# The variance of the last layer norm: from VectorE's statistics to a row sum on VectorE and squares on ScalarE

## The reference

```
x = x + layernorm(attn(layernorm(x)))
x = x + layernorm(ffn(layernorm(x)))

layernorm(h) = (h - mean(h)) / sqrt(var(h) + 1e-5)
ffn(x): h   = gelu(x @ ternary(W1).T + b1)      # 512 -> 2048
        out = h @ ternary(W2).T + b2            # 2048 -> 512
```

## Time and profile before

| | |
|---|---|
| median of three runs | 1421.73 us |
| span of the profiled execution, first to last instruction | 1420.3 us |
| TensorE busy | 1400.8 us, 99% |
| VectorE busy | 1116.8 us, 79% |
| ScalarE busy | 878.2 us, 62% |
| GpSimd busy | 422.3 us, 30% |
| granted TensorE clock | 0.999 of full speed |

### The profile page before, as it was taken

One profiled execution on the slowest core, in us unless ns is written; L12 is line 12 of the kernel. 1 busy time (PEld: TensorE's weight loads), 2 busy tenths in 40 slices (PEclk: granted clock), 3 DMA queues, 4 the chain that ended last, 5 costly groups with the idle time before them and its releaser, 6 DMA issues.

```text
span 1420.3 us, 18989 instructions
## 1 busy us (share of the span) xinstructions
PE 1400.8 (99%) x6506; PEld 640.0 (45%) x6506; DVE 1116.8 (79%) x1889; ACT 878.2 (62%) x1264; POOL 422.3 (30%) x522
## 2 busy tenths in 40 slices
PE   7999999999999999999999999999999999999997
PEld 4444444444444444444444444444444444444443
DVE  7999987868779686796867878677796877998744
ACT  7999665656556565675656756565565656753443
POOL 5234241322314232042331413223142321523221
PEclk9999999999999999999999999999999999999999
DMA  8703221211311122121311203113111221001200
GB/s 245 254 36 90 60 83 20 78 30 38 82 30 60 30 61 59 30 66 25 89 30 31 82 16 82 31 38 82 31 60 30 53 67 30 30 1 30 60 31 30
DMA packets 155984, 82.00 MB, mean 58 GB/s; under 512 B 132720, under 2 KB 132720, under 8 KB 155760
## 3 DMA queue, kind: packets, MB, share of 16 engines
q1 hardware_dynamic: 155888, 80.79, 22.0%
HBM read 31.49 MB, written 16.78 MB: 34 GB/s over the span
## 4 chain that ended last, share of the span: by engine, by line
PE 85%; DVE 4%; issue 3%; POOL 1%; ACT 0%; POOLq 0%; DVEq 0%; ACTq 0%
PE f2b L581 14%; PE f2b L582 14%; PE f1b L552 14%; PE f1b L553 14%; PE misc L520 6%; PE misc L519 6%; PE misc L518 6%; PE misc L533 3%; PE misc L534 3%; PE misc L532 3%; DVE bn L789 1%; DVE vl L865 0%; DVE vl L874 0%; DVE ring L807 0%; POOL rsc L2038 0%
## 5 line engine op out<-in xcount | busy, mean ns | idle before, releaser
L581 PE MATMUL f2b<-w,ring 128*128 128x512 fp8e5 x1004 | 380.5, 379 | 1.2 <-DVE ring L807 0.9
L582 PE MATMUL f2b<-w,ring 128*128 128x512 fp8e5 x1004 | 380.5, 379 | 0.0
L552 PE MATMUL f1b<-x3T,w 128*128 128x512 f16 x960 | 363.8, 379 | 0.1
L553 PE MATMUL f1b<-x3T,w 128*128 128x512 f16 x960 | 363.8, 379 | 0.0
L1610 ACT ACTIVATE ring<-f1b,par 128x512 f32<-128x512 f32 x256 | 175.2, 684 | 227.8 <-PE f1b L553 227.5
L2037 POOL TENSOR_SCALAR ve<-mv 128x4 f32<-128x4 f32 (+2 forms) x89 | 35.4, 398 | 725.5 <-DVE mv L799 725.4
L807 DVE SCALAR_TENSOR_TENSOR ring<-ring,f_sc 128x512 f16<-128x512 f32 x256 | 212.5, 844 | 37.6 <-ACT ring L1620 37.4
L1620 ACT ACTIVATE ring<-ring,f_sc 128x512 f16<-128x512 f32 x256 | 180.1, 710 | 0.0
L518 PE MATMUL misc<-x1T,win_hi 128*128 128x512 f16 x456 | 172.8, 379 | 0.0
L520 PE MATMUL misc<-x1T,win_lo 128*128 128x512 f16 x456 | 172.8, 379 | 0.0
L519 PE MATMUL misc<-x1T,win_hi 128*128 128x512 f16 x456 | 172.8, 379 | 0.0
(11 more groups left out here) (227 smaller groups left out, 2015.3 us busy)
## 6 DMA issues: line engine op xcount, KB each, us to landing
out_dram<-hb SPq DMA_DIRECT2D x64, 256.0 KB, 2.0
xs<-x_dram SPq DMA_DIRECT2D x14, 1024.0 KB, 5.4
ring<-w1t_dram SPq DMA_DIRECT2D x3, 1024.0 KB, 13.2
stage<-w2t_dram SPq DMA_DIRECT2D x3, 1024.0 KB, 8.0
x1T<-tp SPq DMA_TRANSPOSE x68, 3.1
xs<-x_dram SPq DMA_DIRECT2D x4, 256.0 KB, 3.4
stage<-w_in_dram SPq DMA_DIRECT2D x4, 256.0 KB, 5.7
xs<-x_dram SPq DMA_DIRECT2D x2, 512.0 KB, 7.2
```

The lines of the kernel that those rows point to most:

```text
L552: pe.matmul(b[:, :], w, src[:, k, :], start=k == 0, stop=False)
L553: mm = pe.matmul(b[:, :], w, src[:, KC + k, :], start=False, stop=k == KC - 1)
L581: pe.matmul(f2b[q][:, :], h_hi[:, i % H_SLOTS, qs], w2[:, j, :], start=j == 0, stop=False)
L582: mm = pe.matmul(f2b[q][:, :], h_lo[:, i % H_SLOTS, qs], w2[:, j, :], start=False, stop=j == FC - 1)
```

## The change

For all tiles but the last, f_add also writes the sum of each row (accum_out) into f_row. In place of bn_stats and bn_aggr VectorE does f_mean, a 128x1 multiplication of that sum by -1/512, into f_nm. ScalarE does f_square: Square of `hb` with f_nm as bias, so that it squares the centred values. The squares themselves go to a buffer that nobody reads, and their sum per row goes to f_sq. rstd_f takes the variance from f_sq / 512 and the mean from f_nm, in four operations. The squares have the numbers 1.05, 1.07, 1.09 and 2.05 in ScalarE's lists. Those of tile 13 stand at the end of step 15, behind the last gate_hi. The last tile keeps its statistics; the counts that it waits for are changed to match.

```diff
-AT_F_ADD, AT_F_STATS, AT_F_AGGR = 0.0, 0.8, 1.15
+AT_F_ADD, AT_F_MEAN, AT_F_SQUARE = 0.0, 0.25, (1.05, 1.07, 1.09, 2.05)
...
                 ve_.scalar_tensor_tensor(out=hb[:, j, :], in0=f2b[j][:, :], scalar=f_inv[:, 0:1], in1=b2_row,
-                                         op0=ALU.mult, op1=ALU.add).then_inc(f_ok, 1)
+                                         op0=ALU.mult, op1=ALU.add,
+                                         accum_out=f_row[:, j:j + 1] if e < NT - 1 else None).then_inc(f_ok, 1)
...
+            def f_mean(e, j):
+
+                ve_.wait_ge(f_ok, NB * e + j + 1)
+                if e > 0:
+                    ve_.wait_ge(rs_ok[4], e)
+                ve_.tensor_scalar(f_nm[:, j:j + 1], f_row[:, j:j + 1], -1.0 / D, None, ALU.mult).then_inc(fm_ok, 1)
+
             def epilogue(e):
                 return (spread(AT_F_ADD, .2, [lambda j=j: f_add(e, j) for j in range(NB)])
-                        + spread(AT_F_STATS, .1, [lambda j=j: f_stats(e, j) for j in range(NB)])
-                        + spread(AT_F_AGGR, .01, [lambda j=j: aggr(4, e, j) for j in range(NB)]))
+                        + spread(AT_F_MEAN, .2, [lambda j=j: f_mean(e, j) for j in range(NB)]))
...
                     for j in range(NB):
-                        f_stats(NT - 3, j)
+                        f_mean(NT - 3, j)
                         if j < NB - 1:
                             h_add(NT - 1, j + 1)
                         h_stats(NT - 1, j)
-                        aggr(4, NT - 3, j)
...
+            def f_square(e, j):
+
+                i = NB * e + j
+                act.wait_ge(fm_ok, i + 1)
+                if i > 1:
+                    act.wait_ge(fq_ok, i - 1)
+                act.activation(spare[:, j % 2, :], hb[:, j, :], ACT.Square, bias=f_nm[:, j:j + 1],
+                               accum_out=f_sq[:, j:j + 1], saturate=False).then_inc(fq_ok, 1)
...
+                if e is not None and e != NT - 3:
+                    items += [(at, lambda j=j: f_square(e, j)) for j, at in enumerate(AT_F_SQUARE)]
...
                 if s == NT - 1:
                     for b in range(2, KC):
                         gate_hi(NT - 1, b)
+                    for j in range(NB):
+                        f_square(NT - 3, j)
...
-                rstd(4, e, rs4[:, :], False)
-                link(pool.tensor_tensor(tmp4[:, 1, :], mean_var(4)[:, :, 0], rs4[:, :], ALU.mult))
-                link(pool.tensor_tensor(tmp4[:, 2, :], tmp4[:, 1, :], c0[:, e % 4, :], ALU.add))
-                pool.tensor_scalar(nm4[:, :], tmp4[:, 2, :], -1.0, None, ALU.mult).then_inc(rs_ok[4], 1)
+                pool.wait_ge(fq_ok, NB * (e + 1))
+                link(pool.tensor_scalar(ve[:, 4, :], f_sq[:, :], 1.0 / D, EPS, ALU.mult, ALU.add))
+                link(pool.tensor_tensor(rs4[:, :], ve[:, 4, :], mhalf[:, :], ALU.pow))
+                link(pool.tensor_tensor(tmp4[:, 1, :], f_nm[:, :], rs4[:, :], ALU.mult))
+                pool.tensor_tensor(nm4[:, :], tmp4[:, 1, :], c0[:, e % 4, :], ALU.subtract).then_inc(rs_ok[4], 1)
```

More of the change, by code:

```diff
@@ L178, in build @@
         tmp4 = sb("tmp4", [P, 3, NB])
+        f_row = sb("f_row", [P, NB])
+        f_nm = sb("f_nm", [P, NB])
+        f_sq = sb("f_sq", [P, NB])
+        spare = sb("spare", [P, 2, D], F8)
         ones = sb("ones", [P, P])
@@ L250, in build @@
             sem("x1_ok"), sem("n3_ok"), sem("x3_hi"), sem("x3_lo"))
+        fm_ok, fq_ok = sem("fm_ok"), sem("fq_ok")
         f2_sum, fin_last, xc_ok, cen_ok = sem("f2_sum"), sem("fin_last"), sem("xc_ok"), sem("cen_ok")
@@ L785, in stats @@
             def stats(ln, t, j, src):
-                if t > 0:
+                if t > 0 and ln < 4:
                     ve_.wait_ge(mv_ok[ln], NB * (t - 1) + j + 1)
@@ L791, in aggr @@
             def aggr(ln, t, j):
-                ve_.wait_ge(bn_ok[ln], NB * t + j + 1)
+                ve_.wait_ge(bn_ok[ln], (NB * t if ln < 4 else 0) + j + 1)
                 if ln == 0 and t in (1, 2):
@@ L992, in last_centre @@
             def last_centre(j):
-                ve_.wait_ge(mv_ok[4], NB * (NT - 1) + j + 1)
+                ve_.wait_ge(mv_ok[4], j + 1)
                 ve_.tensor_scalar(hb[:, j, :], hb[:, j, :], mean_var(4)[:, j, 0:1], None, ALU.subtract).then_inc(cen_ok, 1)
@@ L2034, in rstd @@
             def rstd(ln, t, dst, last, js=slice(0, NB), done=None):
-                pool.wait_ge(mv_ok[ln], NB * t + js.stop)
+                pool.wait_ge(mv_ok[ln], (NB * t if ln < 4 else 0) + js.stop)
                 link(pool.tensor_scalar(ve[:, ln, js], mean_var(ln)[:, js, 1], EPS, None, ALU.add))
```

## The result

The changed kernel takes 1433.45 us (median of four runs, 1433.3 to 1434.94) against 1421.38 us of the kernel before (four runs as well, 1420.95 to 1422.21). The ratio is 1.0084, with a 95% interval of 1.0071 to 1.0097. The span of its profiled execution is 1433.1 us, 12.8 us more than before. Each execution takes 1.7 to 1.9 us longer than its own span, and the two profiled executions were each the longest or nearly the longest of their four (1434.94 us here; before, a span of 1420.3 belongs to some 1422.1 by that estimate), so the medians differ by less than the spans, by 12.1 us.

A forecast was written before the change was run, and what follows sets the result against it. TensorE, busy 99%, was taken as the bound, slowed only by waits. 10.7 us (tiles 0 to 12) + 1.0 (tile 14) + 0.8 (tile 13 less the wait at 1331) = 12.5: 1434.2 us, range 1431.5 to 1438.

The forecast's parts named there:

- the step S: On ScalarE, start of one square to the next, accumulator read included: taken as 0.71 us, bounds 0.61 and 0.92.
- B: Rival: the squares' accumulator read on ScalarE does not overlap, S = 0.92, 1443.4 us; chance 0.12.
- E: Rival: the squares' accumulator read on ScalarE is hidden, S = 0.61, 1429.7 us; chance 0.10.
- D: Rival: ScalarE's squares are cheap, S under 0.44, slack swallows all four, 1420.4 to 1421.7 us; chance 0.05.
- The wait at f1(4): Three squares ahead of gelu 2 make TensorE wait 0.82 us per step, 10.7 us for tiles 0 to 12.
- Tile 14: In the step beginning at 1357.45, f1(5) follows f1(4) directly, so gelu 3 counts: 1.01 us lost.
- Tile 13: Its squares and the Gelu table load behind them delay gelu 0, so TensorE waits 1.1 us at f1(2).
- The 0.33 us at 1331: TensorE's wait for VectorE at 1331.54, which VectorE's earlier end of its statistics can take away: 0.33 us.
- Rival C: Square is not in Gelu's table, so changes between them load tables, 1.28 us each: about 1491 us; chance 0.03.
- Rival F: The row sum slows VectorE's f_add to 1.4 us, so a square waits for its mean: 1439 us; chance 0.03.
- GpSimd's chain: One operation shorter, from about 347.8 to about 351.1, before ScalarE gets to the norm at about 351.9: no hold-up.
- the stores may come later: Stores go out some 1.5 us later, and hb is wanged again only half a step on: no cost.

## Why the prediction was right, point by point

- The time: 12.5 us and 1434.2 us were forecast, the medians differ by 12.1 and the changed kernel takes 1433.45. The offset of 1.4 us between span and median in the forecast is no property of the kernel: it comes from the profiled execution's being longer than the median one, and it cancelled, because the 12.5 us were in effect added to the median.
- What bounds the kernel: right. TensorE's pitch is unchanged, and the 35.6 us less work on VectorE were worth nothing in the steps (the run with the statistics kept).
- The order of ScalarE's work and the step S = 0.71: right. Squares start 0.71, 0.70 and 0.71 us apart. Rivals B (0.92), E (0.61) and D (under 0.44) are out by this step alone. The run without the read measured 0.61, so the read isn't hidden.
- The wait at f1(4): 0.82 predicted, 0.78 measured, in the 13 steps and in tile 14's. With 2, 3 or 4 in place of the 3 in 3S - 1.31 the formula gives 0.11, 0.82 and 1.53 at S = 0.71, where 0.08, 0.78 and 1.48 were measured. The 0.04 at three squares are gelu 2, which lasts 0.67 here and not 0.69, the lag of 0.05 and not 0.06, and 0.01 between gelu 1 and the first square. The steps are 87.13 us long (f1(4) at 349.18 and the next at 436.31), where 87.15 was forecast.
- Tile 14: 1.01 predicted, 0.93 measured, the second part ahead of f1(5) as worked out.
- Tile 13: 1.1 predicted, 1.05 measured. The wait is gone when the table load is moved ahead of the squares. The 0.33 us at 1331 came back.
- Rival C was out: there are 30 loads ahead of the gelus, as in the earlier trace rows, and 61 in all, as before. No load stands directly ahead of a square: 56 of them run behind a load for the gelus, and the four of tile 13 behind one for the silus. The Trainium skill, page "ScalarE: Activation LUTs", section "Table sets: the hidden batching unit", has cheap functions in every set and doesn't name Square among them. The trace agrees with this rule if Square is one of them, at least in the two sets that this kernel uses here.
- Rival F was out: f_add with its row sum steps in 0.66 to 0.68 us, where it stepped in 0.66 without, and the read is all but hidden.
- VectorE 40 us less busy, ScalarE 43 more: 35.6 and 37.5. The direction was right, and the sizes mean nothing for the time. Other groups of VectorE moved as well, which no run took apart: the taps (line 877) take 118.8 us in place of 105.9, and lo 199.2 in place of 212.5.
- The mis-sized term is GpSimd's chain. I had it done at 351.1, some 0.8 us ahead of ScalarE's norm. It takes as long with four operations (3.84 us) as with five before the change (3.88, from 346.46 to 350.34):

```profile
350.00 0.72 POOL L2091 TENSOR_SCALAR ve<-f_sq 128x4 f32<-128x4 f32 x1 [13.15 <-ACT spare L1645]
350.80 1.39 POOL L2092 TENSOR_TENSOR rs<-ve,mhalf 128x4 f32<-128x4 f32 x1
352.27 0.44 POOL L2093 TENSOR_TENSOR tmp<-f_nm,rs 128x4 f32<-128x4 f32 x1
352.79 1.05 POOL L2094 TENSOR_TENSOR nm<-tmp,c 128x4 f32<-128x4 f32 x1
353.94 1.52 ACT L1651 ACTIVATE hb<-hb,nm,rs 128x512 f32<-128x512 f32 x2
```

The chain runs from 350.00 to 353.84; I had taken 3.3 us. The last operation alone takes 1.05. The margin ahead of the norm was 0.1 us and not 0.8. It cost nothing, and that was luck: an error of 0.7 us fell into a margin of 0.8. The sentence that the stores may come later without harm was luckier than its reasoning, too: 1.5 us later is free, and the run with the norms 3 groups later shows 3 us lost per step. What the prediction should have had there is the chain behind the norm: finish, VectorE's scans and y under it, silu_y, gates.

## What to carry to other kernels

Where one engine is saturated, an edit that moves work between the others is priced by the tightest slack that it is put into, not by busy shares: here 1.31 us per step on an engine that is 62% busy. Count the instructions that an in-order queue puts ahead of the one that the bound engine waits for, times their step from start to start. The same four squares cost 21 us, 12 us or 1.7 us by where they stood, and nothing where only one stood ahead and a table load was moved as well. The slack on the other side, behind the norm, has an end too: norms that came three groups later cost 43 us with no square in the kernel.

## What the runs showed of the hardware that was not expected

- A 128x4 operation of GpSimd takes from 0.20 to 1.07 us for the same work. The subtraction of the chain takes 1.05 us in 12 of 15 tiles of the changed kernel and 0.20 in all 15 of the run with late norms and squares; the product ahead of it takes 1.07 in the run with one square ahead and 0.20 to 0.44 in the changed kernel. VectorE is at work beside it in the slow case shown above, but no run took that apart.
- VectorE's accumulator read (0.08 us) adds about 0.01 us to f_add's step, and ScalarE's (0.19 us) adds 0.09 to a square's.
- VectorE's statistics of 128x512 lasted 0.68 us before, and the square that replaces one lasts 0.71 on ScalarE, without its read: the exchange was about one for one in time.
- In the run with the norms alone a pause of TensorE of 4.4 us was followed by a granted clock of 0.52 over two microseconds; in the two runs with late squares and late norms the same pause was followed by 0.50. The losses of 0.78 and 1.48 us at f1(4) were not: over the whole span the clock was 0.999 in the changed kernel and with four squares ahead.
